# Graph layer on one core: another order of SyncE's list in the node update, and the low part of x1 by a matmul with minus the identity

## The reference

```
Q, K, V = x@Wq, x@Wk, x@Wv            # 8 heads of 32
score   = softmax(Q K^T / sqrt(32))   # 8 x 8 per node, over its own heads
x1      = score @ V
agg     = segment_sum(x1[dst] * x1[src], dst)
h  = layernorm(x + agg@O_w + O_b) * ln1_w + ln1_b
h  = layernorm(h + relu(h@f1_w+f1_b)@f2_w + f2_b) * ln2_w + ln2_b
o  = GRU cell with input h and state h
x  = layernorm(x + o)                                    # "xmid"
h  = x @ W;  e = exp(-leaky_relu(h@a1 [src] + h@a2 [dst]))
out = layernorm(x + relu(segment_sum(e * h[dst], src) / segment_sum(e, src)))
```

## Time and profile before

| | TensorE | weight load | VectorE | ScalarE | GpSimd |
|---|---|---|---|---|---|
| busy us | 2425.1 | 1966.7 | 1954.9 | 1318.5 | 578.7 |
| share of the span | 93% | 75% | 75% | 50% | 22% |

### The profile page before, as it was taken

How to read it: one execution, slowest core, us unless ns; L and a number is a source line. 1 busy time by engine, 2 the same in 40 slices (tenths; PEclk the granted TensorE clock), 3 DMA queues, 4 the chain that set the end, 5 groups by cost and what they waited for, 6 DMA issues and landing times. The chain is left out here.

```text
span 2620.5 us, 46932 instructions
## 1 busy us (share of the span) xinstructions
PE 2425.1 (93%) x16048; PEld 1966.7 (75%) x16048; DVE 1954.9 (75%) x3244; ACT 1318.5 (50%) x2190; POOL 578.7 (22%) x629
## 2 busy tenths in 40 slices
PE   3899969999999999959898889889999999999996
PEld 2566647777777777736565556579999999999996
DVE  5899966666666666637576566589999898989896
ACT  3222338888888888814433334355434334343432
POOL 4698960000000000024243324100001010101010
PEclk9999989999999999979999999989999999999998
DMA  3111102223223222250202111166464545454543
GB/s 99 36 46 44 44 18 120 117 106 132 106 109 129 106 121 117 106 173 29 71 29 71 57 57 43 57 149 145 94 124 90 117 89 124 89 121 89 120 92 71
DMA packets 405991, 239.92 MB, mean 92 GB/s; under 512 B 326288, under 2 KB 397584, under 8 KB 399568
## 3 DMA queue, kind: packets, MB, share of 16 engines
q1 hardware_dynamic: 397536, 228.12, 32.0%
q10 hardware_dynamic: 7056, 6.43, 0.7%
q0 software_dynamic: 1248, 3.41, 0.5%
HBM read 48.38 MB, written 110.84 MB: 61 GB/s over the span
## 5 line engine op out<-in xcount | busy, mean ns | idle before, releaser
L1792 PE MATMUL d_acc<-d_rows_high,d_weights_high 128*128 128x258 f32 x2401 | 682.8, 284 | 6.1 <-DVE d_weights_low L1668 6.1
L1793 PE MATMUL d_acc<-d_rows_low,d_weights_high 128*128 128x258 f32 x2401 | 678.6, 283 | 0.0
L1794 PE MATMUL d_acc<-d_rows_high,d_weights_low 128*128 128x258 f32 x2401 | 678.2, 282 | 0.0
L1422 PE MATMUL b_pagg<-x_parts,b_counts 128*128 128x512 f32 x2401 | 656.4, 410 | 0.5 <-ACT b_counts L1463 0.5
L1742 ACT CAST d_weights_high<-d_weights 128x896 fp32r<-128x896 f32 x343 | 323.4, 945 | 500.9 <-PE d_acc L1794 293.3
L1422 PEld LDWEIGHTS b_pagg<-x_parts,b_counts 128*128 128x128 f32 x2401 | 423.7, 189 | 74.4 <-ACT b_counts L1463 1.1
L1792 PEld LDWEIGHTS d_acc<-d_rows_high,d_weights_high 128*128 128x128 f32 x2401 | 455.3, 190 | 10.2 <-DVE d_weights_low L1668 6.0
L1793 PEld LDWEIGHTS d_acc<-d_rows_low,d_weights_high 128*128 128x128 f32 x2401 | 455.3, 190 | 2.2 <-issue 2.2
L1794 PEld LDWEIGHTS d_acc<-d_rows_high,d_weights_low 128*128 128x128 f32 x2401 | 455.1, 190 | 0.0
L1107 DVE TENSOR_TENSOR b_lo_hot<-b_nodes,b_ends 128x1024 bf16<-128x1024 f16 x392 | 270.9, 691 | 210.9 <-PE b_pcounts L1433 210.5
L1668 DVE TENSOR_TENSOR d_weights_low<-d_weights,d_weights_high 128x896 fp32r<-128x896 f32 x343 | 373.1, 1088 | 52.8 <-ACT d_weights_high L1742 51.2
(11 more groups left out here) (160 smaller groups left out, 2790.4 us busy)
## 6 DMA issues: line engine op xcount, KB each, us to landing
edge_counts<-b_counts SPq DMA_DIRECT2D x49, 1568.0 KB, 5.1
node_table<-u_table SPq DMA_DIRECT2D x7, 903.0 KB, 6.3
qx<-in_x SPq DMA_DIRECT2D x49, 128.0 KB, 2.0
x_table<-x_tile ACTq DMA_DIRECT2D x49, 128.0 KB, 1.7
agg<-b_sums SPq DMA_DIRECT2D x49, 128.0 KB, 4.5
u_x<-x_table SPq DMA_DIRECT2D x7, 896.0 KB, 8.2
u_agg<-agg SPq DMA_DIRECT2D x7, 896.0 KB, 10.1
u_x<-in_x SPq DMA_DIRECT2D x7, 896.0 KB, 5.1
```

Source lines behind the costliest of these rows:

```text
L1422: last = nc.tensor.matmul(pagg[:, o, :], ca[:, o, hi, :], x1_parts[:, hi].rearrange("p m d -> p (m d)"), start=(hi == 0), stop=(hi == TILE ...
L1792: nc.tensor.matmul(acc[:, r, 0:HT], a, high[:, t, :], start=(t == 0), stop=False)
L1793: nc.tensor.matmul(acc[:, r, 0:HT], a, low[:, t, :], start=False, stop=False)
L1794: return nc.tensor.matmul(acc[:, r, 0:HT], b, high[:, t, :], start=False, stop=(t == TILES - 1))
```

## The change

In attention VectorE no longer subtracts. A tile `minus`, minus the identity, is made once. TensorE's step T opens with a matmul of `minus` with the high part of tile T−6, added to the sum that stands in the bank, once `high` says that it is written; ScalarE's step T opens with a copy of what is left in the bank into the low part. In the node update SyncE's list for a group g is now: load of x of g+2, loads of x1 and agg of g+3, and the two stores behind them; the loads of x1 and agg of group 2 stand ahead of the loop. Every wait is for the same event as before.

```
@@ attention_rows
+        minus = sb("minus_ident", [P, P], F32R)
+        minus_ready, less_high = kit.sem("minus_ident_ready"), kit.sem("x1_less_high")
@@ TensorE
                 def step(T, u):
+                    t, s = T - 6, u % 2
+                    if is_tile(t):
+                        if isinstance(T, int) and t == 0:
+                            pe.wait_ge(minus_ready, 1)
+                        pe.wait_ge(high, T - 5)
+                        nc.tensor.matmul(x1_sum[:, s:s + 1, 0:D], minus[:], part(0, t), start=False, stop=True,
+                                         skip_group_check=True).then_inc(less_high, 1)
-                tile_steps(pe, step, 4)
+                tile_steps(pe, step, 6)
@@ ScalarE
                 def step(T, u):
+                    t, s = T - 6, u % 2
+                    if is_tile(t):
+                        act.wait_ge(less_high, T - 5)
+                        nc.scalar.copy(part(1, t), x1_sum[:, s:s + 1, 0:D]).then_inc(low, 1)
-                tile_steps(act, step, 5)
+                tile_steps(act, step, 6)
@@ VectorE
-                    t, s = T - 5, (u - 1) % 2
-                    if is_tile(t):
-                        dve.wait_ge(high, T - 4)
-                        nc.vector.tensor_tensor(part(1, t), x1_sum[:, s:s + 1, 0:D], part(0, t), ALU.subtract).then_inc(low, 1)
-
-                tile_steps(dve, step, 5)
+
+                nc.vector.tensor_scalar(minus[:], c["ident"][:], -1.0, None, ALU.mult).then_inc(minus_ready, 1)
+                tile_steps(dve, step, 2)
@@ update_rows, SyncE
-                sp.wait_ge(attn_ready, GROUP)
+                sp.wait_ge(attn_ready, upto(0, GROUP - 1))
                 load(x1t[:], x1, 1, x1_in)
                 load(agt[:], agg, 1, agg_in)
                 weights.load_rest(nc, sp)
+                sp.wait_ge(attn_ready, upto(1, GROUP - 1))
+                load(x1t[:], x1, 2, x1_in)
+                load(agt[:], agg, 2, agg_in)
                 for g in range(GROUPS):
                     if g + 2 < GROUPS:
-                        sp.wait_ge(attn_ready, upto(g + 1, GROUP - 1))
-                        load(x1t[:], x1, g + 2, x1_in)
-                        load(agt[:], agg, g + 2, agg_in)
                         sp.wait_ge(resid[2], upto(g, GROUP - 1))
                         load(xt[:, g % 2], x, g + 2, x_in)
+                    if g + 3 < GROUPS:
+                        sp.wait_ge(attn_ready, upto(g + 2, GROUP - 1))
+                        load(x1t[:], x1, g + 3, x1_in)
+                        load(agt[:], agg, g + 3, agg_in)
                     sp.wait_ge(xm_ready, upto(g, GROUP - 1))
```

## The result

The changed kernel takes 2566.55 us (median of 4 runs, 2564.77 to 2568.14), beside 2622.67 us for the kernel before in the same comparison: ratio 0.9785, 95% interval 0.9771 to 0.9800. The forecast was 2567 us, with 2559 to 2576 as the range. Measured once more, the same kernel took 2564.76 us.

The account below looks back on a forecast made before the run. TensorE's work plus four bubbles bound the update, a VectorE-TensorE loop attention; 2622.3 − 50.7 (update) − 5.5 (attention) = 2566.1, forecast 2567 us because the runs' median lies 1.5 above the profiled execution; range 2559 to 2576.

Parts of the forecast that it names:

- TensorE's landmark: Node update: transposes of the last two h1 tiles, 68.42 us from one body to the next without a late load.
- the 13.2 us of a bubble: Node update: time lost per body to a late agg load, 13.26, 13.23, 12.85 and 11.39, in all 50.7 us.
- 7.02 + 1.95 = 8.97 us ... Most of the other 4.3 us is clock: Node update: TensorE's idle time per late-load body is 8.97 us; most of the remaining loss is the lower clock.
- the bounds: Node update: saving between 4 × 8.97 = 36 us (idle time alone) and 4 × 13.26 = 53 us.
- rival (b): Node update: another wait or the lower clock remains in each body, saving 36 instead of 50.7: 2582 us; chance 0.08.
- VectorE's lead over the h1 landmark: Node update: VectorE reaches its multiply 12.9 us before TensorE's last h1 transposes, 9.9 a body earlier; no new wait builds up.
- the step without the matmul, 5.46: Attention: TensorE's step without waits, before the new matmul is added, taken as 5.46 us.
- the 0.11 for a gap: Attention: 0.11 us more per tile if a wait ahead of the new matmul opens the gap seen between sum and transposes.
- (a): Attention: TensorE sets the step at 5.8 to 5.95 us, matmul's weight load and wait not hidden: 2571 to 2577; chance 0.13.
- (c): Attention: the step reaches TensorE's 5.57 us because ScalarE's exponential can slip: 2561 us; chance 0.04.
- (d): Attention: new matmul waits in lockstep for ScalarE's high copy, 2636 us; or update stores held back, same sign; chance 0.015.
- (e): Node update: loads still late because the waiting multiply holds them; only attention's gain is left: 2618 us; chance 0.015.

Follow-up runs that it names:

- The list alone: Kernel before with only SyncE's new list in the node update, attention untouched: 2571.59 us beside 2620.12, ratio 0.9813.
- the filled bubble: Kernel before with 15 extra float32 matmuls on TensorE in each of four waits for the last h1 row: 2625.96 us beside 2620.95, ratio 1.0022.
- Gain alone: Kernel before with only the attention part changed and SyncE's old list: 2614.60 us beside 2620.12, ratio 0.9977.
- the kernel with key first and transposes twice: Changed kernel with ScalarE's key copy ahead of its exponential and each tile's two x transposes done twice: 2566.30 us beside 2620.81, ratio 0.9790.
- the key-first kernel: Changed kernel with ScalarE's key copy ahead of its exponential in attention's step: 2555.94 us beside 2620.12, ratio 0.9754.

## Why the prediction was right, point by point

**Update, mechanism and place: right.** Loads of group 3 went at 1256.8, forecast near 1262 less attention's gain; no wait for `agg` beyond the first; stores 68.37 apart against 68.42 read from TensorE's landmark; granted clock 1.00; nothing late next. 50.9 us from the stores against 50.7. The list alone gave 48.5, with an interval of 3 us to each side. That the whole came within 0.5 us of the forecast is in part luck: four executions of the changed kernel spread over 3.4 us.

**Update, where the 13.2 us of a bubble come from: wrong.** The step that failed is "7.02 + 1.95 = 8.97 us ... Most of the other 4.3 us is clock". The sum did not rest on it, since the landmarks count everything, but the bounds (36 us for idle time alone) and rival (b) did. Four more rows of the kernel before, TensorE's timeline, give the right count:

```profile
1236.27 0.38 PE L571 MATMUL u_tp<-ident,u_xmid 128*128 128x128 f32 x2
1236.49 1.89 PE L582 MATMUL u_mo<-f,u_hiddenT 128*128 128x256 f32 x8
1238.22 0.60 PE L640 MATMUL u_tp<-ident,u_nT 128*128 128x128 f32 x4
...
1319.90 0.60 PE L640 MATMUL u_tp<-ident,u_nT 128*128 128x128 f32 x4
```

Without a bubble the xmid transposes follow the h1 landmark by 3.65 us (1232.62 to 1236.27); from 1301.04 that is 1304.69. They ran at 1315.87, 11.18 us late, and this instant is VectorE's: multiply at 1307.63 plus 8.24. The 5.00 us of slow f1 matmuls lie ahead of it and cost nothing. From there to the next landmark it took 4.03 us (1315.87 to 1319.90) instead of 1.95, 2.08 more. 11.18 + 2.08 = 13.26. Of the 2.08 the slow matmuls are 1.4 (3.29 for 1.89), but not all of that need be the clock: in the run with the loads 15 us behind the `xmid` store the same stretch, behind a late load too but at a granted clock of 1.00 (window 1298 to 1304), takes 3.03 (1297.98 to 1301.01). Measured against that, the clock has 1.0 us. So its share of the 13.26 is about a tenth at most, and rival (b) in the form "idle time goes, clock stays" had no mechanism behind it. The rule of the Trainium skill (TensorE: Matmul & The Clock Gate, on HAM oscillation) gave 3.8 us of throttled loss for the window. The trace has 3.0 us of slow work in it (5.00 for 3.37 and 3.29 for 1.89), somewhat less, as TensorE stood idle for 2.25 of the 11.56 us and had no work then to be slowed; and the filled bubble shows that half of this slow work was hidden behind VectorE.

It follows also that a late load does not start to cost at 12.9 us (VectorE's lead over the h1 landmark). The xmid transposes are late from 1288.13 + L + 8.24 = 1304.69 on, L = 8.3, and the work behind them somewhat sooner: bodies with 7.82 and 7.97 us of waiting still lost 0.6 and 0.8 us, those with 9.14 and 9.08 lost 2.0 and 1.9.

**Attention, the new bound: right.** 5.72 us, VectorE with exponential and key copy; moving the key copy out of it gave 8 us. Gain alone 5.5 us measured, 5.5 taken. The periods read are those of ordinary steps. Once in each round of eight steps (the loop of `tile_steps`) one is longer, in both kernels: over a whole round the sums start 5.90 us apart before (212.03 to 259.24) and 5.75 after (178.87 to 224.87). The difference is 0.15 instead of 0.135, so the sum did not suffer.

**Attention, TensorE's own step: mis-sized.** 5.57 to 5.68 forecast, 5.51 measured. The mis-sized terms are the step without the matmul, 5.46, and the 0.11 for a gap; the matmul itself, 0.11, was about right (0.12). The sum over heads, record by record, first in the kernel before, from its second record on, then in the kernel with key first and transposes twice, which has no wait (TensorE's timeline, short windows):

```profile
182.56 2.54 PE L291 MATMUL p_x<-av_products,ident 128*128 128x256 f32 x11
184.94 0.27 PE L268 MATMUL q_tp_and_v<-ident,qx 128*128 128x128 f32 x1
```

```profile
184.62 2.54 PE L300 MATMUL p_x<-av_products,ident 128*128 128x256 f32 x11
...
187.11 0.38 PE L277 MATMUL q_tp_and_v<-ident,qx 128*128 128x128 f32 x2
```

A record takes 0.216 us without a wait (184.40 to 184.62). In the kernel before, 0.29 lie between the first and the second (182.27 to 182.56): 0.07 more, which is there in every sum behind a wait, is listed as no idle time, and has no place in a step without waits. So that step is 5.46 − 0.07 = 5.39. From the second on, 11 records at 0.216 fill the 2.38 us up to the transposes exactly: there is no gap. The 0.11 of the prediction came from this 0.07 and from 12 × 0.213 in place of 12 × 0.216. With the new matmul the same stretch takes 2.49, and the step 5.51, 0.12 more than 5.39: the matmul's own pace, and nothing for its wait. Rivals (a) and (c) were weighed with the wrong number: the gap that spoke for (a) did not exist, and what kept the step above TensorE's was only ScalarE's order, as the key-first kernel shows.

**Rivals (d) and (e).** ScalarE's high part was done before the new matmul wanted it: no wait of TensorE for ScalarE is listed in attention. The stores were not held back.

## What to carry to other kernels

A late input costs what the chain behind it makes of it, not the idle time of the busiest engine: find the next instant at which that engine cannot move, and subtract from it where it would be otherwise. Take a stage's gain from the distance of one landmark in a period that has the wait and one that has not. Read a gap inside an engine's work from single records: a mean pace times a count, taken across a record that still waits, shows gaps that are not there. When a loop is shortened, list every engine's own step and every cross-engine loop, since the next bound may be a mere order of two instructions on an engine that is half idle.

## What the runs showed of the hardware that was not expected

A single-pass matmul of 256 columns with a wait that is already over, put between float32 matmuls and transposes, lengthened TensorE's step by 0.12 us (5.39 to 5.51), about the 0.11 that such matmuls take in a row in the weighing stage; neither its weight load nor its wait added anything that shows. The same 896 KB load of `agg`, counted from its issue to the multiply that waited for it, took 7.2 to 8.5 us in the four bodies of the run in which it left 15 us behind the `xmid` store, and 10.1 to 11.0 in the four of the kernel before, where it left 1.0 us behind the 903 KB table store. That the store is the reason was not tested by itself.
